# Batch 0 of a ViT tower: key stacks turned by TensorE, query stacks by DMA, and the output projection in two halves of its inner dimension

## The reference

```python
h = einsum('bhid,oi,od->bho', x, weighted_sum, weight)
t = layernorm(h)
q, k, v = heads(t @ qkv_w.T + qkv_b)
q, k = unit(rotate(q)), unit(rotate(k))
attn = softmax(einsum('bhqd,bhkd->bhqk', q, k) * 16 ** -0.5)
h = h + merge(einsum('bhqk,bhkd->bhqd', attn, v)) @ out_w.T + out_b
t = layernorm(h)
w = probs * (probs > 0.5)          # probs = sigmoid(t @ Wg + bg)
hid = relu(einsum('td,edh->eth', t, W1) + b1)
h = h + einsum('te,etd->td', w, einsum('eth,ehd->etd', hid, W2) + b2)
```

## Time and profile before

| what | value |
|---|---|
| median of 3 runs | 1947.99 us (1947.15 to 1950.42) |
| the profiled execution's own time | 1948.63 us |
| its span | 1946.8 us |
| PE busy | 1840.2 us, 95% |
| DVE busy | 753.6 us, 39% |
| ACT busy | 1070.7 us, 55% |
| POOL busy | 661.6 us, 34% |

### The profile page before, as it was taken

One profiled execution on the slowest core, in us unless ns is written; L12 is line 12 of the kernel. 1 busy time (PEld: TensorE's weight loads), 2 busy tenths in 40 slices (PEclk: granted clock), 3 DMA queues, 4 the chain that ended last, 5 costly groups with the idle time before them and its releaser, 6 DMA issues.

```text
span 1946.8 us, 31769 instructions
## 1 busy us (share of the span) xinstructions
PE 1840.2 (95%) x12608; PEld 1163.8 (60%) x12608; DVE 753.6 (39%) x1600; ACT 1070.7 (55%) x1645; POOL 661.6 (34%) x559
## 2 busy tenths in 40 slices
PE   5469799999999999999999999999999999999999
PEld 4137444676457754677546764577645775466666
DVE  7866744546014540246213470044601454021001
ACT  2544477545764466554665456644565546655444
POOL 1003422334233342334323343233423334234443
PEclk9689899999999999999999999999999999999999
DMA  4421543434123151231513333133412314122221
GB/s 161 130 98 39 149 144 132 159 120 109 65 81 128 64 130 66 87 120 66 130 66 109 98 91 105 63 112 98 124 52 106 114 66 114 65 87 98 109 91 52
DMA packets 109780, 194.55 MB, mean 100 GB/s; under 512 B 72616, under 2 KB 86464, under 8 KB 93248
## 3 DMA queue, kind: packets, MB, share of 16 engines
q1 hardware_dynamic: 109632, 192.51, 30.6%
HBM read 154.73 MB, written 20.98 MB: 90 GB/s over the span
## 4 chain that ended last, share of the span: by engine, by line
PE 77%; DVE 8%; DMA 4%; ACT 3%; issue 3%; SPq 0%; DVEq 0%; ACTq 0%
PE bank_h L908 28%; PE bank_f L927 10%; PE bank_f L930 9%; PE bank_f L929 9%; PE bank_o L834 5%; PE bank_s L820 4%; PE bank_s L750 3%; PE bank_s L751 3%; PE bank_s L752 3%; DMA kt<-probs 1%; DMA kt<-stack 1%; DVE tmp_b L1038 1%; DVE acc L1150 1%; DMA raw<-in_w_dram 1%; DVE y L948 1%
## 5 line engine op out<-in xcount | busy, mean ns | idle before, releaser
L616 POOL TENSOR_TENSOR hl<-h,hh 128x512 f16<-128x512 f32 x512 | 600.4, 1173 | 1159.6 <-ACT hh L727 722.7
L908 PE MATMUL bank_h<-x,w1s 128*128 128x512 f16 x3072 | 752.5, 382 | 7.6 <-ACT hh L727 7.2
L724 ACT ACTIVATE h<-bank_h,b1s 128x512 f32<-128x512 f32 x512 | 351.3, 686 | 467.0 <-PE bank_h L908 466.9
L927 PE MATMUL bank_f<-w2s,hh 128*128 128x256 f16 x2048 | 561.4, 274 | 14.2 <-DVE acc L1150 14.2
L929 PE MATMUL bank_f<-w2s,hh 128*128 128x256 f16 x2048 | 559.6, 273 | 0.0
L930 PE MATMUL bank_f<-w2s,hl 128*128 128x256 f16 x2048 | 559.5, 273 | 0.0
L908 PEld LDWEIGHTS bank_h<-x,w1s 128*128 128x128 f16 x3072 | 287.8, 99 | 335.5 <-issue 45.6
L727 ACT ACTIVATE hh<-bank_h,b1s 128x512 f16<-128x512 f32 x512 | 350.0, 684 | 0.0
L693 ACT ACTIVATE probs<-bank_s 128x1024 f32<-128x1024 f32 x240 | 246.5, 1027 | 175.3 <-PE bank_s L820 174.2
L927 PEld LDWEIGHTS bank_f<-w2s,hh 128*128 128x128 f16 x2048 | 201.7, 98 | 123.2 <-issue 58.0
L1150 DVE SCALAR_TENSOR_TENSOR acc<-bank_f,gw,acc 128x256 f32<-128x256 f32 x256 | 106.1, 477 | 367.8 <-PE bank_f L930 367.5
(11 more groups left out here) (157 smaller groups left out, 1520.0 us busy)
## 6 DMA issues: line engine op xcount, KB each, us to landing
w1s<-w_parts SPq DMA_DIRECT2D x56, 1024.0 KB, 4.8
w2s<-w_parts SPq DMA_DIRECT2D x56, 1024.0 KB, 4.8
raw<-in_w_dram SPq DMA_DIRECT2D x16, 1024.0 KB, 6.6
xraw<-in_x_t_dram SPq DMA_DIRECT2D x30, 512.0 KB, 4.8
w_parts<-w1s SPq DMA_DIRECT2D x8, 1024.0 KB, 8.7
w_parts<-w2s SPq DMA_DIRECT2D x8, 1024.0 KB, 11.4
out_dram<-acc SPq DMA_DIRECT2D x16, 256.0 KB, 6.0
turned_gates<-maxima_rows SPq DMA_DIRECT2D x6, 192.0 KB, 3.5
```

The costliest lines, as they stand in the source:

```text
L616: pool.tensor_tensor(hl[n % HBUFS][:], h32[n % 2][:], hh[n % HBUFS][:], ALU.subtract)\
L724: act.activation(h32[n % 2][:], bank_h[n % 2][:, :], ACT.Relu, bias=b1s[:, e, m:m + 1]).then_inc(h_hi.sem, 1)
L908: last = pe.matmul(bank_h[n % 2][:, :], w[:, wp, k, m * P:(m + 1) * P], x16s[fb % 2][:, xp, k, :], start=(k == 0 and wp + xp == 0), stop=( ...
L927: pe.matmul(o, high, w[:, 0, m, :], start=(m == 0 and t % 2 == 0), stop=False, skip_group_check=True)
```

## The change

It touches batch 0 only. (1) Stack tiles 2 and 3 get buffers of their own, in the space of `w1s1`, which is not yet in use; the waits of ACT and DVE for the turns fall away there. (2) SP turns only the queries by DMA. The keys are turned on PE, eight 128x128 f16 transposes for a tile (`key_turn`) into the banks `bank_f`, by an identity that POOL copies to `hl0`, and ACT copies them to `kt` (`key_copy`). (3) The output projection goes by halves of its 256 inner rows: `att_half 0` and `project_half 0` take the first 128, which is head groups 0 and 1, and stand between the scores; `att_half 1` and `project_half 1` come at the end. All four tiles are in one step, and the sums stay in `bank_f` from one half to the other.

```diff
@@ -68,7 +68,8 @@
                  "rotate 2", "qkv 3", "rotate 3", "qk_norm 0", "unit 0", "unit 1", "stack 0", "unit 2", "stack 1",
-                 "unit 3", "stack 2", "stack 3", "projections 1"]
+                 "key_turn 0", "key_copy 0", "unit 3", "stack 2", "key_turn 1", "key_copy 1", "stack 3", "key_turn 2",
+                 "key_copy 2", "key_turn 3", "key_copy 3", "projections 1"]
         steps = [(0.1 * k, name.split()[0], int(name.split()[1])) for k, name in enumerate(early)]
@@ -83,6 +84,11 @@
                   (tail + 8.5 + 0.8 * t, "logits", t)]
+    if alone:
+        steps = [s for s in steps if s[1] not in ("att_turn", "project")]
+        steps += [(first + PACE * 22.5, "att_half", 0), (first + PACE * 24.5, "project_half", 0),
+                  (tail, "att_half", 1), (tail + 1.1, "project_half", 1)]
     steps += [(tail + 5.2, "ln2", 0), (tail + 11.2, "gates", 0), (tail + 12.7, "gates_turn", 0),
@@ -255,6 +261,10 @@
                   .rearrange("p (a h s d) -> p a h s d", a=2, h=HEADS, s=4)]
+        more_stacks = w1s[1][:].rearrange("p a k n -> p (a k n)").rearrange("p (i a h s d) -> p i a h s d", i=2, a=2,
+                                                                            h=HEADS, s=4)
+        att_h = [xh[:, 4 * k:4 * k + 4] for k in range(DK)]
+        att_l = [xl[:, 4 * k:4 * k + 4] for k in range(DK)]
         squares = [probs[0][:, t, :] for t in range(TT)]
@@ -346,6 +356,7 @@
         stack_ready = signal("stack_ready", 2 * TT)
+        keys_turned = sem("keys_turned")
         stack_turned = [signal(f"stack_turned{a}", 16 * TT) for a in range(2)]
@@ -411,10 +422,18 @@
-        def stack_slots(t, a):
-            stack_t = stacks[t % 2]
+        def key_bank(t):
+            return bank_f[t % 2][:, :].bitcast(F16).rearrange("p (h t) -> p h t", t=P)
+        def stack_of(b, t):
+            return more_stacks[:, t - 2] if b == 0 and t >= 2 else stacks[t % 2]
+        def stack_slots(b, t, a):
+            stack_t = stack_of(b, t)
             high, low = ((stack_t[:, 0, :, 0:4:2, :], stack_t[:, 0, :, 1:4:2, :]) if a == 0 else
@@ -540,14 +559,14 @@
                 for t in tiles:
-                    for a in range(2):
+                    for a in range(2 if b else 1):
                         wait(sp, stack_ready, b, 2 * t + a + 1)
...
                         sp.dma_start_transpose((qt, kt)[a][:, :, t * P:(t + 1) * P],
-                                               stacks[t % 2][:, a].rearrange("p h s d -> p (h s d)"))\
+                                               stack_of(b, t)[:, a].rearrange("p h s d -> p (h s d)"))\
                           .then_inc(stack_turned[a].sem, 16)
@@ -640,6 +659,7 @@
             pool.wait_ge(consts_in, 16 * 8)
+            pool.tensor_copy(hl[0][:, 0:P], ident[:]).then_inc(pool_consts, 1)
             run(pool, steps)
@@ -681,10 +701,13 @@
                         wait(act, weighed, ab, 0)
-                        if n >= 2:
+                        if n >= 2 and ab:
                             wait(act, stack_turned[a], ab, 16 * (n - 1))
-                        high, _, unit_qk = stack_slots(n, a)
+                        high, _, unit_qk = stack_slots(ab, n, a)
                         copy(high, unit_qk).then_inc(stack_hi.sem, 1)
+                elif stage == "key_copy":
+                    act.wait_ge(keys_turned, n + 1)
+                    copy(kt[:, :, n * P:(n + 1) * P], key_bank(n)).then_inc(stack_turned[1].sem, 16)
                 elif stage == "scores":
@@ -702,6 +725,9 @@
                     copy(turned_h[:, n % 2], tile_ps[n % 2]).then_inc(att_hi.sem, 1)
+                elif stage == "att_half":
+                    wait(act, att_turned, ab, 2 * (n + 1))
+                    copy(att_h[n], turn_ps).then_inc(att_hi.sem, 2)
                 elif stage == "ln2_turn":
@@ -807,6 +833,17 @@
                     last.then_inc(qkv_done.sem, 1)
+                elif stage == "key_turn":
+                    if n == 0:
+                        pe.wait_ge(pool_consts, 2)
+                    else:
+                        wait(pe, stack_turned[1], ab, 16 * (n - 1))
+                    wait(pe, stack_ready, ab, 2 * n + 2)
+                    for h in range(HEADS // 2):
+                        last = pe.transpose(key_bank(n)[:, h, :],
+                                            stack_of(ab, n)[:, 1, 2 * h:2 * h + 2].rearrange("p h s d -> p (h s d)"),
+                                            hl[0][:, 0:P])
+                    last.then_inc(keys_turned, 1)
                 elif stage == "scores":
@@ -839,6 +876,8 @@
                     wait(pe, att_out, ab, n)
+                    if fb is None and n == 2:
+                        wait(pe, att_lo, ab, 2)
                     wait(pe, ln1_lo, ab, TT)
@@ -850,6 +889,26 @@
                     turn(att_turned, n, lambda k: att[:, n, k * P:(k + 1) * P])
+                elif stage == "att_half":
+                    wait(pe, att_out, ab, 2 * (n + 1))
+                    for t in range(TT):
+                        last = pe.transpose(turn_ps[:, t, :], att[:, t, n * P:(n + 1) * P], ident[:])
+                    last.then_inc(att_turned.sem, 2)
+                elif stage == "project_half":
+                    wait(pe, att_hi, ab, 2 * (n + 1))
+                    wait(pe, att_lo, ab, 2 * (n + 1))
+                    pe.wait_ge(set_lo, 4)
+                    for t in range(TT):
+                        o = bank_f[t // 2][:, t % 2 * D:(t % 2 + 1) * D]
+                        pe.matmul(o, att_h[n][:, t, :], outw[:, 0, n, :], start=(n == 0 and t % 2 == 0), stop=False,
+                                  skip_group_check=True)
+                        pe.matmul(o, att_h[n][:, t, :], outw[:, 1, n, :], start=False, stop=False,
+                                  skip_group_check=True)
+                        last = pe.matmul(o, att_l[n][:, t, :], outw[:, 0, n, :], start=False, stop=(n == DK - 1),
+                                         skip_group_check=True)
+                        if n == DK - 1:
+                            last.then_inc(projected.sem, 1)
                 elif stage == "project":
@@ -1062,9 +1121,9 @@
                     for a in range(2):
-                        high, low, unit_qk = stack_slots(n, a)
+                        high, low, unit_qk = stack_slots(ab, n, a)
                         wait(dve, stack_hi, ab, 2 * n + a + 1)
-                        if n >= 2:
+                        if n >= 2 and ab:
                             wait(dve, stack_turned[a], ab, 16 * (n - 1))
@@ -1083,6 +1142,20 @@
                        .then_inc(att_lo.sem, 1)
+                elif stage == "att_half":
+                    wait(dve, att_hi, ab, 2 * (n + 1))
+                    dve.tensor_tensor(att_l[n], turn_ps, att_h[n].bitcast(F32), ALU.subtract).then_inc(att_lo.sem, 2)
+                elif stage == "project_half" and n == DK - 1:
+                    wait(dve, resid_biased, ab, 1)
+                    accn = accs[ab % 2]
+                    for s in range(2):
+                        wait(dve, projected, ab, 2 * (s + 1))
+                        rows = [a[:, 2 * s:2 * s + 2, :].rearrange("p t d -> p (t d)") for a in (accn, resid)]
+                        dve.tensor_tensor(rows[0], bank_f[s][:, :], rows[1], ALU.add).then_inc(h2_out.sem, 2)
+                        wait(dve, h2_out, ab, 2 * (s + 1))
+                        for t in (2 * s, 2 * s + 1):
+                            ins = dve.bn_stats(stats[:, t].rearrange("p h s -> p (h s)"), accn[:, t, :])
+                        att_v.link(dve, ins)
                 elif stage == "project":
```

## The result

The changed kernel takes **1956.9 us** (median of 6 runs, 1954.75 to 1958.51), the kernel before 1948.64 in the runs beside it (6 runs, 1947.15 to 1950.42): ratio 1.0038, 95% interval 1.0028 to 1.0049. It is 8.3 us slower where 7.5 were forecast. The profiled execution took 1955.5 around a span of 1953.7, which is 6.9 above the one shown before.

The account below looks back on a forecast made before the run. Bounds in batch 0: the DMA key turns before the first scores, then ACT's exponentials setting the pace. Exponential 25 8.2 late plus 0.3 of cold, less 1.0 at the tail: +7.5 on 1947.99, 1955.5 us; range 1950.0 to 1959.5.

Parts of the forecast that it names:

- Scores earlier by 1.25: Start of batch 0: with keys turned on PE, the first scores begin at 69.1, 1.25 us earlier.
- Key turns at 1.4, last copy at 65.2: PE and ACT at the start: eight transposes take 1.4 us per tile, the last key copy ends at 65.2.
- Rival 2: Dear key turns: the eight transposes don't overlap, 3.6 us a turn, 6.65 more than the sum, 1962; chance 0.06.
- DVE's weight work late by 0.85: DVE's subtraction behind ACT's output weights copy begins 0.85 us late, and this goes through to group 1's normalisation.
- Stall of 4.8 at att_half 0: PE, between scores 22 and 23, waits 4.8 us for DVE's normalisation of head group 1.
- Second wait 0.6: PE waits 0.6 us at project_half 0 for DVE's low half, which stands behind weight parts 6 and 7.
- Cold projection, 2.6: First projection half on PE: twelve matmuls at half clock take 2.6 us, against 1.45 warm.
- Tail 1.0 gained: End of batch 0's attention: group 3's transposes to last statistics take 6.0 us, 1.0 us gained.
- Carried to the end unchanged: The +7.5 us where layer norm 2 begins stays the same to the end, through fixed orders on every engine.
- Rival 3: The short stall: key turns of 0.8 and a clock that stays up, +4.5, 1952.5; included in the likeliest case's 0.72.
- rival 4: Taken back later: shifted pauses behind layer norm 2 return up to 4 of the 7.5 us, 1951.5; chance 0.10.
- Rival 1: No stall, not slower: DVE finishes group 1 before PE comes to att_half 0, 1947.8; chance 0.12.

Follow-up runs that it names:

- e4: The changed kernel with weight parts 6 and 7 moved behind the low half of att_half 0; 1958.02 us.
- e2: Only the projection in halves, against the kernel before; keys turned by DMA through two stack buffers as before; 1957.25 us.
- e3: The changed kernel with the output weights split right behind stack 1, not behind the last key copy; 1955.57 us.
- e1: Only the key turns on TensorE and the four stack buffers, against the kernel before; projection whole at the end; 1948.76 us.
- e5: The changed kernel with weight parts 4 to 7 moved behind scores 24; 1951.08 us.
- e7: The changed kernel with weight parts 4 to 7 behind scores 24 and the output weights split right behind stack 1; 1949.59 us.

## Why the prediction was right, point by point

- **Scores earlier by 1.25: mechanism right, the term too small.** It was 2.0 (68.30). I had kept the 3.32 per tile of the earlier trace rows; without a key turn between them the first three query turns are issued 3.22 and 3.12 apart (55.76, 58.98, 62.10). The last begins at 62.10 + 4.33 - 1.24 = 65.19, 0.6 before my 65.80, and lands after 3.1 and not 3.2; the scores follow at once, without the 0.1 that I had added.
- **Key turns at 1.4, last copy at 65.2: too high.** A turn of eight took 1.01 to 1.03, near my lower bound, and the last copy ended at 64.75. Rival 2 (3.6 a turn) is out. Taken as eight times the 275 to 390 ns that the Trainium skill, TensorE: Matmul & The Clock Gate, section "Part 4: PE-mode transpose", gives for one bf16 transpose, a turn would be an estimated 2.2 to 3.1; the rows here, in f16 and at half clock (granted 0.50 from 56 to 64), show less than half of that.
- **DVE's weight work late by 0.85: the chain right, its start mis-sized.** The subtraction began at 65.30, 0.32 late, since the output weights' copy came at 64.65 and not 65.2. From there the lateness did go through the load that follows parts 3, and its rows on SP's queue, before and after, show 0.21 of it:

```profile
82.25 0.38 SPq L509 DMA_DIRECT2D raw<-in_w_dram  x1
82.46 0.38 SPq L528 DMA_DIRECT2D raw<-in_w_dram  x1
```

  The maxima began at 89.19 for 88.99, the normalisation at 97.41 for 97.21, both 0.20 late. The longer wait in front of the maxima, 3.86 for 1.19, is no delay: group 0's normalisation came 2.5 earlier (82.36 for 84.82), so that DVE was ready sooner for a load that was not. My lower bound, 0.45 early with turns of 0.8, was wrong by my own steps: stack 3's keys are ready at 62.75 whatever a turn takes, so a turn 0.6 shorter leaves the subtraction 0.27 late.
- **Stall of 4.8 at att_half 0: right, 5.58.** PE came 1.36 earlier than forecast (92.59), DVE was through 0.64 earlier (98.11): 4.8 + 1.36 - 0.64 = 5.5. Of PE's 1.36, 0.8 are the scores' earlier start; the clock also rose sooner (granted 0.73 from 72 to 76, 0.50 before).
- **Second wait 0.6: 0.81**, worth nothing by itself (e4). The profile puts it down to "issue", but it ended at 102.78, 0.1 behind the end of DVE's low half (102.00 + 0.68).
- **Cold projection, 2.6: wrong here.** It ran from 102.78 to 104.38 with the clock back up. In e2, e3 and e4 it was cold, so both bounds occur. With DVE 0.64 early this makes exponential 25 only 6.4 late (104.84), not 8.2.
- **0.3 for what is left of the cold: 0.1.** The transposes of the projection's input came 6.44 later (115.75 for 109.31), exponential 25 6.36.
- **Tail 1.0 gained: 0.4.** From the transposes of the projection's input to the end of the statistics it took 6.63 (115.75 to 122.38) against 7.06 (109.31 to 116.37). The clock fell at 118.5 in the middle of the second half, whose last matmuls start 0.21 apart.
- **Carried to the end unchanged: right for the changed kernel's trace** (+6.0 at layer norm 2, 125.92 for 119.90; +6.2 at the last store), **wrong as a rule.** e1, e3, e4, e5 and e7 each lost 1.4 to 2.3 us between layer norm 2 and the store of the maxima.

So the traces show some 6 to 7 us where the medians show 8.3. The second trace of the changed kernel, with the slow pair, ended 1 us later by the count above and took 1957.43. That the median lies above the first trace because such executions are frequent is argued, not shown. The forecast of 7.5 is closer to 8.3 than its terms deserve, and that is luck: up to layer norm 2 its terms give 1.5 too much (exponential 25 by 1.8, the cold by 0.2, the tail 0.6 the other way), and for what the clock may do behind batch 0 it has nothing.

Rival 3's warm projection and short key turns came about, its short stall did not; rival 4, time given back later, did not either. Rival 1, no stall, is what e7 builds; it measures 1949.59 to the 1947.8 that I gave it, and both are no change within what can be told. The mechanism, DVE's queue at the new place, is what the experiments bear out.

## What to carry to other kernels

A step put into the middle of an in-order engine's list waits until its input is there, and that hour is set by what stands ahead in the queue of the engine that makes the input. Before moving a step earlier, read that queue at the new place: here two weight parts, which had held nobody up, stood between the input and its new reader and two more before the second input, and moving the four behind both gave back 5.6 of 8.3 us (e5). The length of the wait is not its price: once the engine that sets the pace has run dry, the moved work is paid too, and so is a lower clock behind the wait (e2: 2.56 us of stall, 7.5 us lost). And a gain at the start of a long program is not yet a gain at its end: read the same mark at several later places before counting it.

## What the runs showed of the hardware

- **A lead can be lost to the clock without any wait.** Both traces of e1 come to the next batch's first mix over 2 us early and run it at half clock. Windows of e1:

```profile
133.00:140.00 7.00, 4.73 (x14) 2.04 (x13) 4.46 (x5) 2.89 (x5) 0.44 (x1) 0.50 0.00 0
140.00:145.00 5.00, 5.00 (x25) 4.96 (x26) 0.92 (x2) 0.63 (x1) 1.25 (x1) 0.53 0.30 105
```

  and of the kernel before, where the clock is up in the second:

```profile
133.00:140.00 7.00, 4.92 (x14) 2.06 (x14) 4.00 (x8) 2.23 (x5) 0.00 (x0) 0.53 0.00 0
140.00:145.00 5.00, 4.05 (x30) 3.44 (x31) 2.35 (x5) 1.93 (x4) 1.70 (x1) 1.00 0.32 108
```

  PE did almost the same in the seven microseconds before. Why the clock comes back at about 140 in the kernel before and at about 145 in e1 is open.
- **A DVE instruction stretches while GpSimd works on a large tile.** The timelines of DVE and POOL of the changed kernel: the form that took 1.28 above takes 3.27 beside POOL's addition (78.58 to 81.35). In e3 POOL's addition begins 3.3 us earlier, at 75.33, and there the step beside it stretches, a TENSOR_SCALAR of 2.87 us for 0.75. What the two share is not shown.

```profile
79.16 3.27 DVE L1247 SCALAR_TENSOR_TENSOR w2s<-raw,scl,w2s 128x1024 f16<-128x1024 f32 x1
```

```profile
78.58 2.77 POOL L657 TENSOR_TENSOR resid<-resid,outb 128x1024 f32<-128x1024 f32 x1 [7.60 <-issue]
```
